# Sorting stage: 16-bit comparison of the low one-hot rows, laid out by value then tile, and five items of target-order rows moved to the head of the first graph layer

## The reference, cut to what matters

```python
src = jnp.concatenate([_s, _d, _loop])
dst = jnp.concatenate([_d, _s, _loop])
...
edge_index = jnp.stack([src, dst])
x = x + _L0_gnn_ref(_layernorm(x, axis=-1), edge_index, ...)      # reads x at the ends of the first 3125 edges
x = x + _L0_ffn_ref(...)
x = x + _L1_gnn_ref(_layernorm(x, axis=-1), edge_index, edge_attr_256, ...)   # sums over dst
...
x = x + _L2_gnn_ref(_layernorm(x, axis=-1), edge_attr_20, ..., edge_index)    # sums over src
```

## Time and profile before

| | |
|---|---|
| median of 3 runs | 4573.2 us (4557.44 to 4575.55) |
| the profiled execution, its own time | 4556.39 us |
| its span, first to last instruction | 4553.7 us |
| busy share of the span: PE, DVE, ACT, POOL | 80%, 63%, 38%, 55% |
| sorting stage, from the trace | 0 to 486.9 us |
| first graph layer | 486.9 to 632.6 us |

### The profile page before, as it was taken

How to read it: one execution, slowest core, us unless ns; L and a number is a source line. 1 busy time by engine, 2 the same in 40 slices (tenths; PEclk the granted TensorE clock), 3 DMA queues, 4 the chain that set the end, 5 groups by cost and what they waited for, 6 DMA issues and landing times. The chain is left out here.

```text
span 4553.7 us, 75488 instructions
## 1 busy us (share of the span) xinstructions
PE 3662.9 (80%) x20890; PEld 2937.3 (65%) x20890; DVE 2884.9 (63%) x6152; ACT 1716.4 (38%) x3863; POOL 2495.2 (55%) x2542
## 2 busy tenths in 40 slices
PE   5889369888999999835299999479999668878288
PEld 4666257677788888633188888367777556666165
DVE  8887449358889989762288888333333445555753
ACT  2657232302333333312166777233333223333132
POOL 5787547667777777466377777200000277776300
PEclk9755569999999999957599999779999878888589
DMA  8456426449999999745378888320000167777400
GB/s 199 141 181 206 135 79 202 130 148 311 327 339 335 337 334 337 236 103 151 118 227 242 244 248 246 99 66 0 0 0 0 52 182 206 214 207 202 116 15 28
DMA packets 661731, 790.40 MB, mean 174 GB/s; under 512 B 151811, under 2 KB 584051, under 8 KB 657812
## 3 DMA queue, kind: packets, MB, share of 16 engines
q1 hardware_dynamic: 369553, 300.43, 22.5%
q0 software_dynamic: 117920, 308.04, 22.3%
q10 hardware_dynamic: 174083, 179.76, 12.6%
HBM read 516.89 MB, written 275.42 MB: 174 GB/s over the span
## 5 line engine op out<-in xcount | busy, mean ns | idle before, releaser
L1593 POOL DMA_INDIRECT by_dst<-dst_row,place x416 | 462.0, 1111 | 167.1 <-issue 112.9
L2824 POOL DMA_INDIRECT fl_far<-x_table,fl_index x416 | 445.1, 1070 | 150.8 <-issue 126.5
L2212 POOL DMA_INDIRECT a_far<-kv_table,a_index x416 | 424.5, 1020 | 150.2 <-issue 117.7
L2547 POOL DMA_INDIRECT a_far<-src_table,a_index x416 | 415.5, 999 | 131.9 <-issue 120.2
L3657 POOL DMA_INDIRECT starts<-p_out,p_at x25 | 24.6, 984 | 705.0 <-DMA starts<-p_zero 697.0
L2861 PE MATMUL ps<-fl_w,fl_hid 128*128 128x256 f32 x1664 | 398.0, 382 | 14.8 <-ACT ps L2933 12.9
L2246 PE MATMUL ps<-a_w,a_edge_t 128*128 128x256 f32 x1664 | 396.6, 382 | 0.0
L2861 PEld LDWEIGHTS ps<-fl_w,fl_hid 128*128 128x128 f32 x1664 | 309.2, 190 | 59.6 <-issue 19.6
L2246 PEld LDWEIGHTS ps<-a_w,a_edge_t 128*128 128x128 f32 x1664 | 302.2, 192 | 33.0
L1220 ACT ACTIVATE f_hid<-ps,f_bn 128x320 f32<-128x320 f32 x320 | 197.5, 617 | 327.5 <-PE ps L1174 327.5
L1261 DVE SCALAR_TENSOR_TENSOR x_sb<-ps,f_cw,x_sb 128x256 f32 x200 | 96.8, 484 | 343.4 <-PE ps L1185 343.4
(11 more groups left out here) (581 smaller groups left out, 9363.2 us busy)
## 6 DMA issues: line engine op xcount, KB each, us to landing
partial<-a_out ACTq DMA_DIRECT2D x208, 546.0 KB
a_edge<-by_dst SPq DMA_DIRECT2D x104, 516.0 KB
partial_f<-fl_out ACTq DMA_DIRECT2D x26, 2056.0 KB, 10.1
dst_row<-in_edge_attr SPq DMA_DIRECT2D x52, 1024.0 KB
xn_sb<-q_table SPq DMA_DIRECT2D x416, 128.0 KB
fl_keys<-key_rows SPq DMA_DIRECT2D x26, 1024.0 KB, 5.1
a_keys<-local_rows SPq DMA_DIRECT2D x104, 128.0 KB
m_far<-kv_table SPq DMA_DIRECT2D x15, 640.0 KB, 7.2
```

What stands on the lines that cost most here:

```text
L1593: self.nc.gpsimd.indirect_dma_start(out=self.table, out_offset=bass.IndirectOffsetOnAxis(ap=self.place[:, n:n + 1], axis=0), in_=self.row[ ...
L2212: gathered[b % 4].count(nc.gpsimd.indirect_dma_start(out=far[:, b, u, :], out_offset=None, in_=kv_table, in_offset=bass.IndirectOffsetOnAx ...
L2547: gathered[b].count(nc.gpsimd.indirect_dma_start(out=far[:, b, u, :], out_offset=None, in_=src_table, in_offset=bass.IndirectOffsetOnAxis( ...
L2824: gathered[q * 4 + t // 4].count(nc.gpsimd.indirect_dma_start(out=far[:, q, t, :], out_offset=None, in_=table, in_offset=bass.IndirectOffs ...
```

## The change

Three edits. The low part of the keys is kept as 16-bit floats (`split_lo`), compared with a 16-bit table `every_lo` of 128 values x 8 tiles that is written once, and the one-hot rows are laid out by value and then tile, so that the eight tiles of a value are neighbours. The stationary operand of a count matmul is thus read with a step of 8 elements (16 bytes) instead of 1. The high part stays as it was, in a tensor of its own. Five of the 30 items of the sorting stage move to the head of the first graph layer, in front of its narrow items on POOL; on SP the first four narrow loads stay ahead of the wide ones. Line numbers of the changed kernel are higher by 2 to 7.

```diff
-def l0_gnn_stage(core, xt, early, first_rows, share, base, count, ends, windows, local_rows):
+def l0_gnn_stage(core, xt, early, first_rows, by_dst, by_src, base, count, ends, windows, local_rows):
...
                 for g in range(1, GROUPS):
                     load_far(sp, 0, g)
-                share.load(sp)
+                by_src.begin(sp)
+                by_dst.load(sp)
+                by_src.load(sp)
                 sp.wait_ge(local_stored, 16)
...
-                share.scatter(pool)
-                share.finish(pool)
+                by_dst.scatter(pool)
+                by_src.scatter(pool)
+                by_src.finish(pool)
...
-        split = st.sb("split", [P, 2, 2, ETILES])
-        lo_hot = st.sb("lo_hot", [P, 2, 8, P], BF16)
+        split_lo, split_hi = st.sb("split_lo", [P, 2, ETILES], BF16), st.sb("split_hi", [P, 2, ETILES])
+        every_lo = st.sb("every_lo", [P, P, 8], BF16)
+        lo_hot = st.sb("lo_hot", [P, 2, P, 8], BF16)
...
-                        last = nc.tensor.matmul(ps[:, HIST[h % 2], m * W:HB].rearrange("p (n a) -> p n a", a=W), lo_hot[:, h % 2, m, :],
+                        last = nc.tensor.matmul(ps[:, HIST[h % 2], m * W:HB].rearrange("p (n a) -> p n a", a=W), lo_hot[:, h % 2, :, m],
...
-                ch.link(nc.vector.tensor_copy(split[:], cut))
+                ch.add(nc.vector.tensor_copy(split_lo[:], cut[:, 0]))
+                ch.add(nc.vector.tensor_copy(split_hi[:], cut[:, 1]))
+                ch.settle()
+                ch.add(nc.vector.tensor_copy(every_lo[:], core.c("iota").unsqueeze(2).broadcast_to([P, P, 8])))
...
-                    nc.vector.tensor_tensor(lo_hot[:, h % 2], core.c("iota").unsqueeze(1).broadcast_to([P, 8, P]),
-                                            split[:, 0, s, g * 8:g * 8 + 8].unsqueeze(2).broadcast_to([P, 8, P]), ALU.is_equal).then_inc(lo_made, 1)
+                    nc.vector.tensor_tensor(lo_hot[:, h % 2], every_lo[:], split_lo[:, s, g * 8:g * 8 + 8].unsqueeze(1).broadcast_to([P, P, 8]),
+                                            ALU.is_equal).then_inc(lo_made, 1)
...
-                place_stage(core, a["x"], a["consts"], (a["dst"], a["src"]), base, count, place, keys_f, ends, dst_rows.share(30), packing, first_rows)
+                place_stage(core, a["x"], a["consts"], (a["dst"], a["src"]), base, count, place, keys_f, ends, dst_rows.share(25), packing, first_rows)
...
-                        l0_gnn_stage(core, xt, early, first_rows, src_first.share(99), base, count, ends, windows, local_rows)
+                        l0_gnn_stage(core, xt, early, first_rows, dst_rows.share(5), src_first.share(99), base, count, ends, windows, local_rows)
```

More of the change, by code:

```diff
@@ L1950, in make_hot @@
                         dve.wait_ge(counted, h - 1)
-                    nc.vector.tensor_tensor(lo_hot[:, h % 2], core.c("iota").unsqueeze(1).broadcast_to([P, 8, P]),
-                                            split[:, 0, s, g * 8:g * 8 + 8].unsqueeze(2).broadcast_to([P, 8, P]), ALU.is_equal).then_inc(lo_made, 1)
+                    nc.vector.tensor_tensor(lo_hot[:, h % 2], every_lo[:], split_lo[:, s, g * 8:g * 8 + 8].unsqueeze(1).broadcast_to([P, P, 8]),
+                                            ALU.is_equal).then_inc(lo_made, 1)
                     nc.vector.tensor_tensor(hi_hot[:, h % 2], core.c("iota25").unsqueeze(1).broadcast_to([P, 8, W]),
-                                            split[:, 1, s, g * 8:g * 8 + 8].unsqueeze(2).broadcast_to([P, 8, W]), ALU.is_equal).then_inc(hi_made, 1)
+                                            split_hi[:, s, g * 8:g * 8 + 8].unsqueeze(2).broadcast_to([P, 8, W]), ALU.is_equal).then_inc(hi_made, 1)
                 def find_begins(s):
@@ L2006, in _ @@
                             ch.add(nc.vector.tensor_tensor(hit[:, h % 2], core.c("iota25").unsqueeze(1).broadcast_to([P, 8, W]),
-                                                           split[:, 1, s, g * 8:g * 8 + 8].unsqueeze(2).broadcast_to([P, 8, W]), ALU.is_equal))
+                                                           split_hi[:, s, g * 8:g * 8 + 8].unsqueeze(2).broadcast_to([P, 8, W]), ALU.is_equal))
                     if s == 0:
```

## The result

The changed kernel took 4516.5 us (median of 4 runs, 4512.15 to 4527.28) and the kernel before 4574.4 us (4557.44 to 4576.48) on the same chip: a ratio of 0.9885, 95% interval 0.9854 to 0.9916. The profiled execution took 4520.46 us, against 4556.39 us before.

A forecast was written before the change was run, and what follows sets the result against it. DVE bounds the count part, DVE and TensorE nearly both the s = 0 loop, TensorE the s = 1 loop, POOL the sorting stage's end. -27.1 + 3.3 - 12.5 - 12.0 + 1.2 = -47.1 us; forecast 4514 us, range 4476 to 4547.

The forecast's parts named there:

- POOL's last narrow scatter behind DVE's last add: First graph layer: a sign that the forecast is wrong; it expected POOL's last landing at 142 us, DVE at 144.7.
- The boundary: End of the sorting stage: with five items moved it ends with DVE instead of POOL, 27.1 us gained.
- The comparison's price: 16-bit comparison on DVE: 690 ns in place of 1219 for 1024 elements, 0.53 us less per group.
- The count part: Count part of the sorting stage: TensorE at 1.2 GHz becomes the bound, 1.17 us a group, 12.5 us gained.
- the rival on the clock: Count part and loop of s = 0: TensorE's clock rises, DVE bounds both; -77.8 us in total, 4479 us, chance 0.13.
- The loop of s = 0: Sorting stage's first loop: TensorE needs 3.42 us of the 3.58 us period; 12 us gained, bounds 8.3 to 27.6.
- Stepped loads: TensorE's weight loads with a step of 16 bytes: hidden or 10 ns longer, counted as nothing.
- both rivals on it: TensorE's stepped loads: 25 ns each, total -27.6 us, chance 0.11; or 0.1 us each, total +31 us, chance 0.07.
- the loop then gains nothing: Loop of s = 0 in the rival with stepped loads at 25 ns each: +2 us there, 4529 us, chance 0.11.
- The graph layer: First graph layer with five items added: 3.3 us lost to slower far loads, bounds 0 and 12 us.
- The far loads' part: Head of the first graph layer: wide scatters and 1 MB loads slow the far loads, 3.3 us taken.
- POOL ends last: First graph layer: POOL ends after DVE by up to 12 us; total -35 us, 4521 us, chance 0.07.

The follow-up runs named there:

- Experiment 1: Kernel before with only the five items moved to the first graph layer, old comparison and layout kept; 0.991 of before (0.9895 to 0.9926).
- experiment 7: Changed kernel with 16-bit table and rows laid out by tile then value, weights contiguous, key repeated innermost; 0.9958 of before, 4561.2 us.

## Why the prediction was right, and where it was not

The number was close (4514 forecast, 4516.5 measured), but partly by luck: two errors of 12 and 13 us in the first two stages cancelled, and one of the prediction's own signs of being wrong came true, POOL's last narrow scatter behind DVE's last add.

- **The boundary.** I took 27.1 us for the stage's end moving to DVE. Experiment 1: 27.0 us. In executions with the long gather it is worth 18.7 us more, which the one profile I had did not contain. That would account for ratios of 0.985 on the later chips in place of 0.9885. Whether the slower of the first runs of before (4573 to 4576 us against 4557) had it too is open.
- **The comparison's price.** 690 ns forecast, 695 measured, and 1216 with a step of 0 innermost. The rule of the Trainium skill ("VectorE: DVE Perf Modes", section "The perf-mode tier table"), two elements a cycle, agrees with the 695 ns; that it doesn't hold with a step of 0 innermost is experiment 7.
- **The count part: the step that failed.** I kept TensorE at its lower level, as "at that level a group with transposes takes some 0.42 us for these and 0.82 us for its eight matmuls", and got 12.5 us. The sum was right for that level, 2.34 us forecast and 2.30 measured for two groups. What failed is that the level stays: with eight matmuls at 0.71 us two groups take 1.89 us for most of the part, and the measured gain is 21.2 us (79.1 to 57.9). This is the rival on the clock, for a part of its ground; the loop of s = 1 stayed at 0.50 as the forecast had it.
- **The loop of s = 0.** 12 us forecast, 16.4 in the first profile (200.0 to 183.6) and 23.0 in the second (93.5 to 270.4 us, at a clock of 0.69), within its bounds of 8.3 to 27.6. But it was made otherwise than I wrote. At the lower level two periods take 7.09 us, 3.54 each, with TensorE busy for 39.00 of 39.00 us (121 to 160 us), and not 3.42: nearly nothing is gained on 3.57. At the higher level a period takes 3.04 us, the bound of DVE. So the gain is nearly all the clock's: 23 periods of 3.04 us in the first profile, 35 in the second.
- **Stepped loads.** 5 ns each at the lower level; at the higher 0.71 against the 0.61 us of the earlier trace rows, 12 ns each, a little over the "10 ns longer" that I allowed. As totals both rivals on it fell. But "the loop then gains nothing", the mark of the smaller one, is what the loop does at the lower level. How much of the 0.12 us between 3.42 and 3.54 the stepped loads take is not shown: 5 ns a load give 0.04, and no run has the fast comparison with contiguous loads.
- **The start.** 1.2 us forecast, 1.3 measured (21.25 against 19.93 us for the first comparison).
- **The graph layer: the step that was mis-sized most.** I gave it 3.3 us and it took 15.4. The far loads' part was about right: DVE ended 147.3 us behind the boundary, against 145.1 before (486.5 to 631.6); over the other profiles, with and without wide items, it varies from 144.8 to 149.4. But POOL's last scatter, forecast to have landed at 142 us, was issued at 149.8 and had landed at 152.2: the narrow ones took 1.49 us each, since more of them fell beside DVE's long mixing at the end, up to 2.29 us each. And I left out the drain of POOL at the stage's end altogether. It stood in the trace of before, 5.27 us long and hidden, so it cost nothing there. This was the rival "POOL ends last", at 13 us instead of up to 12.

At the layer's end the profile showed 48.2 us where the sum said 47.1: 13 us too little for the sorting stage, 12 too little for the layer's loss.

## What to carry to other kernels

When work is moved to an idle engine in the next stage, count how it ends as well as how it runs: in this layer POOL came to the barrier a drain later, and the drain grew with every indirect transfer issued. Move only as many as make the old stage end with its real bound; here three would have done, and five cost the layer 12 us and more, though the two totals can't be told apart. Where a sum depends on TensorE's clock, work it out at both levels, as the level can change when the work gets denser. And take a second profile of the kernel before: one profile can lack a wait that others have.

## What the runs showed of the hardware

- POOL's drain at the end of the first graph layer took 45 ns + 81.7 ns x the indirect transfers of that stage, though the narrow ones had all landed. In the sorting stage (250 to 290 transfers, the 50 gathers counted) the drain ended only 2.5 to 8.6 us behind POOL's last scatter, so the line doesn't hold there; why stays open.
- A gather on POOL lasted 30.4 to 32.0 us in three of six profiles with the 1.22 us comparison, and each time it ended 1.2 us behind the last of DVE's unbroken row of comparisons in the count part. No gather took over 4.5 us in the eight profiles with the 0.69 us comparison, whose DVE paused for 4 us and more in the count part. That DVE holds the gather is argued from this and not shown. The Trainium skill ("SBUF — State Buffer", section "Who interferes with whom") has a DVE instruction with two inputs in SBUF contend with a GpSimd instruction that reads SBUF, over a read interface that they share. Waiting for one such instruction would take about 1.2 us; the 31.7 us span 22 groups. What kept POOL waiting from one to the next was not found.
- TensorE's level: in the changed kernel's count part eight count matmuls took 0.71 us in stretches where DVE fed it a group every 0.94 us, and 0.91 us throughout in the kernel before, with a group every 1.41 us. The granted clock in the profile's rows was 1.00 beside either.
- The same 16-bit comparison takes 695 ns with a key row of eight neighbours repeated outside and 1216 ns with a key repeated innermost.
